# Three buffers for a unit's first weights, and the fourth chunk's routing spread over more units, in the first expert layer of an eight-block network

## The chip, the cores and the metric

The kernel runs on one core of one Trainium2 chip. A core has five engines with their own instruction queues: TensorE (PE, matmuls, with a separate row PEld for weight loads), VectorE (DVE), ScalarE (ACT), GpSimd (POOL) and SyncE (SP, which here only issues DMAs). They wait for one another by semaphores. The metric is the device time of one launch in microseconds (us), lower is better.

## The reference

Four pairs of attention and feed-forward layers work on 32 x 128 = 4096 tokens of width D = 128. The change lies in the first feed-forward layer, which mixes, normalises and routes each token to the best 2 of 8 experts:

```python
n = layer_norm(x, g1, be1)
x = res + n + (n @ mix_w + mix_b)
res = x
n = layer_norm(x, g2, be2)
probs = softmax(n @ router_w)
topw, topi = top_k(probs, 2)
combine = sum(one_hot(topi, E) * topw[..., None], axis=1)
h = silu(einsum('td,edf->tef', n, w1) + b1)
y = einsum('tef,efd->ted', h, w2) + b2
out = res + einsum('te,ted->td', combine, y)
```

## The kernel before

`routed_ffn` computes only the chosen experts. The 32 blocks of 128 tokens form four chunks of 8 blocks (chunks 0 to 3), and two chunks form a part, so that there are two parts. For a chunk, the routing is: VectorE scales the rows (`scale`), TensorE turns them (`turn_z`) and multiplies them by the mixing weights (`mix`), VectorE adds, takes statistics (`mix`, `statistics_1`), GpSimd makes the inverse deviation (`inverse_deviation`), VectorE normalises (`add_x1`, `normalise`, which writes the tile `r`), TensorE turns r (`turn_r`) and makes the logits (`logits`), VectorE and ScalarE make the softmax and pick two experts (`below_max`, `exponent`, `choose_first`, `choose_second`), TensorE counts the tokens before each (`count`), and VectorE makes of this the row of each token (`locate`). GpSimd then scatters the rows of r to these slots in device memory (`scatter`, 16 indirect DMAs for a chunk; those of chunks 2 and 3 wait after every four for the earlier ones to land).

When both chunks of a part are located, `table(p)` works out on VectorE which expert and which rows each unit of the part has. A unit is 256 slots of one expert; a part has 23 units, so there are 46 in all (0 to 45). `out_rows(c)` works out from where the results of chunk c are to be gathered.

A unit u costs: a load of its rows `xe` by SP (`load`, issued 5 units ahead, six buffers; the first load of a part waits for `table_done` and for all the part's scatters to land), a turn on TensorE (`turn_slots`), a copy to `xT` on ScalarE, a copy of the expert's first weights to the tile `w1_u` on VectorE (`copy_w1`, which reads the expert's number into a register first), the matmuls of `hidden` into h_bank, the activation on ScalarE, the matmuls of `result` into the single bank `y_bank`, and on VectorE `copy_y`, which adds the bias and writes `ye`; SP stores it. `result(u)` waits until `copy_y(u-1)` has left the bank. `hidden(u)` waits for `copy_w1(u)`.

The order on each engine is written out by hand. Routing of chunks 0 to 2 comes first (the head, HEAD = 3). `table(0)` and `copy_w1(0)`, `copy_w1(1)` stand in VectorE's queue between the routing of chunk 1 and that of chunk 2. Then comes the loop over units. In turn u of it TensorE does `hidden(u+1)`, `turn_slots(u+3)`, a piece of chunk 3's routing, `result(u)`; VectorE does `copy_w1(u+2)`, `copy_y(u)`, and then a piece of chunk 3's routing:

```python
for u in range(last_unit):
    if u + 2 < last_unit:
        expert[u + 2] = copy_w1(u + 2)
    copy_y(u, expert[u])
```

The pieces go by turn: `scale` in 0, `mix` and `statistics_1` in 2 and 3, both `add_x1` and `normalise` in 4, `turn_r` in 5, `logits` and `below_max` in 6, the choices in 7 and 8, `count` and `locate` in 9 (LAG), `table(1)` and `out_rows(0)` in 10, `out_rows(1)` in 11, `out_rows(2)` and `out_rows(3)` in 21 and 22. From turn 25 on VectorE also adds gathered results of part 0. What is left of the gathering is done in the attention layer that follows.

Of the kernel before, what the change touches and what calls it, by code (L numbers as in the profile page):

```python
# [1502 lines left out]
def routed_ffn(nc, core, name, w1, w1_loaded, w2_dram, b1, router_w, norms, mix_w, mix_b_dram, b2_dram, slots_in, slots_out, late):  # L1503
# [14 lines left out]
    LAG = 9  # L1518
# [11 lines left out]
    with ctx:  # L1530
# [58 lines left out]
        w1_u = [sb(f"w1_u{i}", [D, FC * 128]) for i in range(2)]  # L1589
# [94 lines left out]
        def _(pool):  # L1684
# [60 lines left out]
            scatter(2, 0, 8)  # L1745
            inverse_deviation(3)
            scatter(2, 8, 2 * RT)
# [4 lines left out]
        def _(dve):  # L1752
# [93 lines left out]
            def table(p):  # L1846

                first, last = PARTS[p]
                n, at = unit_counts[p], first_units[p]
                per_u = lambda v: v[:, None, :].to_broadcast([S, n, NE])  # L1850
                per_e = lambda v: v[:, :, None].to_broadcast([S, n, NE])
                numbers = core.iota_units[:, 0:n]
                hit = passed[:, 0:n, :]
                own.link(dve.tensor_tensor(held[:, :], base[:, last, :], begins[:, p, :], ALU.subtract))
                own.did(dve.tensor_scalar(lim[:, :], held[:, :], -float(UT), 0.0, ALU.add, ALU.max))
                own.link(dve.tensor_tensor(square[:, :, :], held[:, :, None].to_broadcast([S, NE, MOST]),
                                           steps[:, None, :].to_broadcast([S, NE, MOST]), ALU.is_gt))
                own.link(dve.tensor_reduce(units[:, :], square[:, :, :], AX.X, ALU.add))
                own.link(dve.tensor_tensor(square[:, :, 0:NE], upto[:, :, :],
                                           units[:, None, :].to_broadcast([S, NE, NE]), ALU.mult))  # L1860
                own.link(dve.tensor_reduce(ends[:, :], square[:, :, 0:NE], AX.X, ALU.add))
                own.link(dve.tensor_tensor(hit, per_u(ends[:, :]), per_e(numbers), ALU.is_le))
                own.link(dve.tensor_reduce(which[:, 0:n], hit[:, :, 0:NE - 1], AX.X, ALU.add))
                own.link(dve.tensor_tensor(hit, hit, per_u(ends[:, :]), ALU.mult))
                own.link(dve.tensor_reduce(begun[:, 0:n], hit[:, :, 0:NE - 1], AX.X, ALU.max))
                own.did(dve.tensor_copy(expert_of[:, at:at + n], which[:, 0:n]))
                own.did(dve.tensor_tensor(begun[:, 0:n], numbers, begun[:, 0:n], ALU.subtract))
                own.link(dve.tensor_tensor(hit, per_u(core.iota8[:, :]), per_e(which[:, 0:n]), ALU.is_equal))
                own.link(dve.tensor_tensor(hit, hit, per_u(lim[:, :]), ALU.mult))
                own.link(dve.tensor_reduce(row[:, 0:n], hit, AX.X, ALU.add))  # L1870
                own.did(dve.tensor_scalar(which[:, 0:n], which[:, 0:n], float((last - first) * REGION),
                                          float(first * NE * REGION), ALU.mult, ALU.add))
                own.link(dve.scalar_tensor_tensor(row[:, 0:n], begun[:, 0:n], float(UT), row[:, 0:n], ALU.mult, ALU.min))
                own.link(dve.tensor_tensor(row[:, 0:n], row[:, 0:n], which[:, 0:n], ALU.add))
                own.link(dve.tensor_copy(row_of[:, at:at + n], row[:, 0:n]))
                own.did(dve.scalar_tensor_tensor(terms[:, p, 2, :], units[:, :], float(UT), lim[:, :], ALU.mult, ALU.subtract))
                own.did(dve.tensor_tensor(terms[:, p, 1, :], lim[:, :], begins[:, p, :], ALU.add))
                own.link(dve.tensor_tensor(terms[:, p, 0, :], ends[:, :], units[:, :], ALU.subtract))
                own.did(dve.tensor_scalar(terms[:, p, 2, :], terms[:, p, 2, :], -float(UT), None, ALU.add))
                own.link(dve.scalar_tensor_tensor(terms[:, p, 0, :], terms[:, p, 0, :], float(UT), begins[:, p, :],  # L1880
                                                  ALU.mult, ALU.subtract))
                dve.sem_inc(table_done, 1)
# [17 lines left out]
            def copy_w1(u):  # L1900
                dve.wait_ge(table_done, part_of_unit[u] + 1)
                e = dve.value_load(expert_of[0:1, u:u + 1], min_val=0, max_val=NE - 1)
                if u >= 2:
                    dve.wait_ge(h_ready, 2 * (u - 1))
                dve.tensor_copy(w1_u[u % 2][:, :], w1[:, bass.ds(e * (FC * 128), FC * 128)]).then_inc(w1_copied, 1)
                return e
# [39 lines left out]
            for c in range(HEAD):  # L1946
                for g in (2 * c, 2 * c + 1):
                    mix(g)
                    statistics_1(g)
                add_x1(2 * c)  # L1950
                add_x1(2 * c + 1)
                statistics(2 * c + 2)
                normalise(2 * c)
                normalise(2 * c + 1)
                statistics(2 * c + 3)
                below_max(c)
                if c + 1 < HEAD:
                    scale(2 * c + 2)
                choose_first(c)
                choose_second(c)  # L1960
                if c + 1 < HEAD:
                    scale(2 * c + 3)
                locate(c)
                if c + 1 == PARTS[0][1]:
                    table(0)
                    dve.wait_ge(w1_loaded, 16 * NE)
                    expert = {0: copy_w1(0), 1: copy_w1(1)}
            dve.wait_ge(b2_loaded, 16)
            for u in range(last_unit):
                if u + 2 < last_unit:  # L1970
                    expert[u + 2] = copy_w1(u + 2)
                copy_y(u, expert[u])
                for c in BEGIN:
# [7 lines left out]
                    if since == 4:  # L1981
                        add_x1(2 * c)
                        normalise(2 * c)
                        add_x1(2 * c + 1)
                        normalise(2 * c + 1)
                    if since == 6:
                        below_max(c)
                    if since == 7:
                        choose_first(c)
                    if since == 8:  # L1990
# [18 lines left out]
        def _(act):  # L2009
# [50 lines left out]
            for u in range(last_unit):  # L2060
# [4 lines left out]
                for c in BEGIN:  # L2065
# [4 lines left out]
                    if since == 5:  # L2070
                        copy_r(2 * c)
                        copy_r(2 * c + 1)
                    if since == 6:
                        exponent(c)

        @block.tensor
        def _(pe):
# [102 lines left out]
            for u in range(last_unit):  # L2180
# [4 lines left out]
                for c in BEGIN:  # L2185
# [925 lines left out]
```

## Time and profile before

| | |
|---|---|
| median of 3 runs | 1486.42 us (1482.06 to 1490.42) |
| profiled execution, its own time | 1486.32 us |
| its span in the trace | 1484.5 us |
| TensorE busy | 1184.3 us (80% of the span) |
| VectorE busy | 991.8 us (67%) |
| ScalarE busy | 667.6 us (45%) |
| GpSimd busy | 537.8 us (36%) |
| mean granted TensorE clock | 0.886 |

Times in the rows are us from the span's start. A busy share is a mean over stages with different limits, so the stage of the change has to be read by itself. "Granted clock" is the share of TensorE's full clock that it was given. The first expert layer begins at about 232 us; its unit loop on TensorE goes from about 332 to 527 us. In a timeline row the bracket tells how long the engine was idle before the instruction and what ended the wait.

### The profile page before, as it was taken

What the parts mean: (1) busy time and instruction counts of PE and PEld (TensorE: products, weight loads), DVE (VectorE), ACT (ScalarE), POOL (GpSimd) and SP (SyncE); (2) the same over time, 40 slices, a digit from 0 to 9 for tenths busy, and PEclk for the clock granted to TensorE, in tenths of its full rate; (3) what the DMA queues carried; (4) which work ended last, traced back from release to release, by engine and by line L of the source; (5) the groups of instructions that cost most, each with busy time, mean ns of one, the idle gap of its engine ahead of it and who ended that gap; (6) DMA issues with size and microseconds to landing.
All of it is one profiled execution on the core that took longest, in us unless ns stands there. A gap on an engine that the chain in (4) does not pass through costs nothing. (4 is left out here: it accounts for less than half of the span.)

```text
span 1484.5 us, 34946 instructions
## 1 busy us (share of the span) xinstructions
PE 1184.3 (80%) x11154; PEld 926.2 (62%) x11154; DVE 991.8 (67%) x2920; ACT 667.6 (45%) x1423; POOL 537.8 (36%) x590
## 2 busy tenths in 40 slices
PE   2799994349899957789987879999799956399991
PEld 1577773238799934566674456677477746389991
DVE  3699885564533346989974678889477777756552
ACT  1377771115455503346554546666243343144440
POOL 2323302663305256635411233431121124752554
PEclk9999995559999966889988989999799988599996
DMA  7887733012223248534532086674200042133442
GB/s 179 211 212 196 186 105 127 29 51 65 78 79 106 85 119 205 135 100 130 155 91 51 19 191 157 152 170 106 85 1 0 0 150 64 54 119 107 147 141 74
DMA packets 138979, 164.58 MB, mean 111 GB/s; under 512 B 15309, under 2 KB 118755, under 8 KB 131729
## 3 DMA queue, kind: packets, MB, share of 16 engines
q1 hardware_dynamic: 130664, 146.62, 36.7%
q0 software_dynamic: 8192, 16.46, 4.0%
q8 instruction: 60, 0.98, 0.3%
q14 instruction: 63, 0.51, 0.1%
HBM read 111.98 MB, written 51.38 MB: 110 GB/s over the span
## 5 line engine op out<-in xcount | busy, mean ns | idle before, releaser
L586 DVE TENSOR_REDUCE A_neg_max<-A_s_bank 128x4 f32<-128x512 f32 x384 | 253.4, 688 | 45.0 <-PE A_s_bank L725 34.5
L448 ACT ACTIVATE A_probsT<-A_st_bank 128x512 f32<-128x512 f32 x384 | 222.2, 602 | 37.9 <-PE A_st_bank L738 36.9
L725 PE MATMUL A_s_bank<-A_k_stack,A_q_stack 72*128 72x128 bf16 x1536 | 158.9, 229 | 37.3 <-DVE A_neg_max L586 23.6
L738 PE MATMUL A_st_bank<-A_q_stack,A_k_stack 128*128 128x128 bf16 x1536 | 153.4, 224 | 7.0 <-DVE A_q_stack L602 6.2
L738 PEld LDWEIGHTS A_st_bank<-A_q_stack,A_k_stack 128*128 128x128 bf16 x1536 | 113.0, 104 | 51.7 <-issue 42.3
L725 PEld LDWEIGHTS A_s_bank<-A_k_stack,A_q_stack 72*128 72x128 bf16 x1536 | 107.2, 102 | 51.7 <-DVE A_neg_max L586 34.1
L752 PE MATMUL A_pv_bank<-A_probsT,A_v_pad 128*32 128x128 f32 x3072 | 128.3, 285 | 0.1
L2043 ACT ACTIVATE E_h<-E_h_bank,w_L_b 128x256 f32<-128x256 f32 x184 | 77.0, 472 | 82.0 <-PE E_h_bank L2143 80.8
L2143 PE MATMUL E_h_bank<-E_xT,E_w_u 128*128 128x256 f32 x368 | 91.4, 394 | 6.1 <-issue 6.1
L2155 PE MATMUL E_y_bank<-E_w,E_h 128*128 x736 | 90.3, 276 | 2.2 <-ACT E_h L2043 1.0
L752 PEld LDWEIGHTS A_pv_bank<-A_probsT,A_v_pad 128*32 128x32 f32 x3072 | 74.6, 111 | 23.5 <-issue 2.2
L2155 PEld LDWEIGHTS E_y_bank<-E_w,E_h 128*128 128x128 f32 x736 | 85.9, 192 | 3.3 <-issue 3.2
L461 ACT COPY A_outT<-A_pv_bank 128x512 f32<-128x512 f32 x99 | 58.0, 586 | 65.9 <-PE A_pv_bank L752 65.8
L2417 POOL DMA_INDIRECT E_yg<-slots_out,E_index_out x64 | 61.5, 960 | 63.9 <-DMA slots_out<-E_ye 29.5
L1912 DVE TENSOR_TENSOR E_ye<-E_y_bank,E_b 128x256 f32<-128x256 f32 x46 | 19.5, 424 | 95.2 <-PE E_y_bank L2155 95.1
L1714 POOL DMA_INDIRECT routed_in<-E_r,E_index x64 | 63.3, 989 | 51.7 <-DVE E_index L1844 27.6
L310 POOL TENSOR_TENSOR A_split_r<-A_k_f,A_k_parts 128x512 f32<-128x512 f32 (+1 forms) x21 | 26.1, 1242 | 151.0 <-ACT A_k_parts L472 75.4
L2402 POOL DMA_INDIRECT slots_in<-E_xn,E_index x64 | 64.0, 999 | 44.1 <-issue 16.9
L2143 PEld LDWEIGHTS E_h_bank<-E_xT,E_w_u 128*128 128x128 f32 x368 | 69.4, 199 | 14.9 <-issue 6.6
L602 DVE COPY A_q_stack<-A_max_rows 32x2048 bf16<-32x2048 bf16 x96 | 70.0, 729 | 2.7
L767 PE MATMUL A_t_bank<-ident,A_outT 128*128 128x128 f32 x396 | 66.6, 293 | 4.8 <-ACT A_outT L461 4.8
L2565 DVE COPY E_w_u<-exp_w 128x512 f32 x53 | 23.6, 448 | 59.9 <-PE E_v_bank L2779 52.3
(371 smaller groups left out, 2658.5 us busy)
## 6 DMA issues: line engine op xcount, KB each, us to landing
A_q_stack<-q_scratch SPq DMA_DIRECT2D x48, 576.0 KB
A_k_stack<-k_scratch SPq DMA_DIRECT2D x32, 576.0 KB
q_scratch<-A_q_parts SPq DMA_DIRECT2D x48, 192.0 KB
A_k_stack<-k_scratch SPq DMA_DIRECT2D x48, 192.0 KB
E_xe<-slots_in SPq DMA_DIRECT2D x53, 128.0 KB
slots_out<-E_ye SPq DMA_DIRECT2D x53, 128.0 KB, 1.7
A_ctxT<-in_ctxT SPq DMA_DIRECT2D x24, 256.0 KB, 10.0
k_scratch<-A_k_parts SPq DMA_DIRECT2D x32, 192.0 KB
```

Source lines behind the costliest of these rows:

```text
L448: act.activation(probsT[n % 2][:, c * HQ:(c + 1) * HQ, :], st_bank[c % 2][:, :].rearrange("k (a q) -> k a q", a=HQ), ACT.Exp, scale=scale) ...
L586: dve.tensor_reduce(neg_max[:, c * HQ:(c + 1) * HQ], s_bank[c % 2][:, :].rearrange("q (a k) -> q a k", a=HQ), AX.X, ALU.max, negate=True). ...
L602: dve.tensor_copy(q_stack[n // 2 % 4][MAX_ROWS, 0:BY_DVE, n % 2 * S:(n % 2 + 1) * S], max_rows[n % 2][MAX_ROWS, None, :].to_broadcast([2 * ...
L725: last = pe.matmul(s_bank[c % 2][:, a * S:(a + 1) * S], q_stack[slot][0:COMBO, h, at:at + S], k_stack[slot][0:COMBO, h, at:at + S], start= ...
L738: last = pe.matmul(dst, k_stack[slot][:, h, at:at + S], q_stack[slot][:, h, at:at + S], start=True, stop=spread)
L752: last = pe.matmul(pv_bank[a * VW:(a + 1) * VW, c * S:(c + 1) * S], v_pad[p][:, n % GB, h % vheads, :], probsT[n % 2][:, h, :], start=True ...
L767: last = pe.transpose(t_bank[:, a * S:(a + 1) * S], outT[:, a, :], core.ident[:, :])
L1714: pool.indirect_dma_start(out=slots_in[:, :], out_offset=bass.IndirectOffsetOnAxis(index[:, k, b:b + 1], 0), in_=r[:, b, :], in_offset=Non ...
L2043: last = act.activation(h[u % 2][:, f, :], h_bank[(2 * u + q) % HB][:, f % 2 * UT:(f % 2 + 1) * UT], ACT.Silu, bias=b1[:, bass.ds(e * FC + ...
L2143: last = pe.matmul(dst, w1_u[u % 2][:, f * 128:(f + 1) * 128], xT[u % 3][:, :], start=True, stop=True)
L2155: last = pe.matmul(y_bank[:, j * D:(j + 1) * D], h[u % 2][:, f, j * S:(j + 1) * S], w2[:, bass.ds(e * (FC * D) + f * D, D)], start=(f == 0 ...
L2402: pool.indirect_dma_start(out=slots_in[:, :], out_offset=bass.IndirectOffsetOnAxis(index[:, k, b:b + 1], 0), in_=xn[:, b, :], in_offset=No ...
```

## The change

The weights tile `w1_u` gets three buffers, `copy_w1` runs three units ahead of `copy_y` in place of two, and three copies in place of two stand in the head. The wait of a copy is for the same turn's `hidden` as before. Of chunk 3, the second `add_x1` and `normalise` go to turn 5, and each later step of the routing goes one turn later, up to `locate` in turn 10. `table(1)` is cut in three pieces for turns 11, 12 and 13; `out_rows` of the four chunks go to turns 14, 15, 20 and 21. GpSimd issues 12 in place of 8 scatters of chunk 2 ahead of chunk 3's inverse deviation. No arithmetic is added or taken away. The operations of `table` are the same, in the same order.

```diff
@@ -1515,7 +1515,8 @@
-    LAG = 9
+    LAG = 10
+    WBUF = 3
@@ -1586,7 +1587,7 @@
-        w1_u = [sb(f"w1_u{i}", [D, FC * 128]) for i in range(2)]
+        w1_u = [sb(f"w1_u{i}", [D, FC * 128]) for i in range(WBUF)]
@@ -1742,9 +1743,9 @@
             scale_of_z(3)
-            scatter(2, 0, 8)
+            scatter(2, 0, 12)
             inverse_deviation(3)
-            scatter(2, 8, 2 * RT)
+            scatter(2, 12, 2 * RT)
@@ -1843,7 +1844,7 @@
-            def table(p):
+            def table(p, pieces=(0, 1, 2)):
...
+                if 0 in pieces:
+                    own.link(dve.tensor_tensor(held[:, :], base[:, last, :], begins[:, p, :], ALU.subtract))
...
+                    own.link(dve.tensor_reduce(ends[:, :], square[:, :, 0:NE], AX.X, ALU.add))
+                if 1 in pieces:
+                    own.link(dve.tensor_tensor(hit, per_u(ends[:, :]), per_e(numbers), ALU.is_le))
...
+                    own.did(dve.tensor_tensor(begun[:, 0:n], numbers, begun[:, 0:n], ALU.subtract))
+                if 2 in pieces:
+                    own.link(dve.tensor_tensor(hit, per_u(core.iota8[:, :]), per_e(which[:, 0:n]), ALU.is_equal))
...
+                    dve.sem_inc(table_done, 1)
@@ -1900,9 +1904,9 @@
-                if u >= 2:
-                    dve.wait_ge(h_ready, 2 * (u - 1))
-                dve.tensor_copy(w1_u[u % 2][:, :], w1[:, bass.ds(e * (FC * 128), FC * 128)]).then_inc(w1_copied, 1)
+                if u >= WBUF:
+                    dve.wait_ge(h_ready, 2 * (u - WBUF + 1))
+                dve.tensor_copy(w1_u[u % WBUF][:, :], w1[:, bass.ds(e * (FC * 128), FC * 128)]).then_inc(w1_copied, 1)
@@ -1964,11 +1968,11 @@
-                    expert = {0: copy_w1(0), 1: copy_w1(1)}
+                    expert = {u: copy_w1(u) for u in range(WBUF)}
             dve.wait_ge(b2_loaded, 16)
             for u in range(last_unit):
-                if u + 2 < last_unit:
-                    expert[u + 2] = copy_w1(u + 2)
+                if u + WBUF < last_unit:
+                    expert[u + WBUF] = copy_w1(u + WBUF)
                 copy_y(u, expert[u])
@@ -1978,28 +1982,22 @@
-                    if since == 4:
-                        add_x1(2 * c)
-                        normalise(2 * c)
-                        add_x1(2 * c + 1)
-                        normalise(2 * c + 1)
-                    if since == 6:
+                    if since in (4, 5):
+                        add_x1(2 * c + since - 4)
+                        normalise(2 * c + since - 4)
+                    if since == 7:
                         below_max(c)
-                    if since == 7:
+                    if since == 8:
                         choose_first(c)
-                    if since == 8:
+                    if since == 9:
                         choose_second(c)
                     if since == LAG:
                         locate(c)
-                if u == BEGIN[NR - 1] + LAG + 1:
-                    table(1)
-                    out_rows(0)
-                if u == BEGIN[NR - 1] + LAG + 2:
-                    out_rows(1)
-                if u == BEGIN[NR - 1] + LAG + 12:
-                    out_rows(2)
-                if u == BEGIN[NR - 1] + LAG + 13:
-                    out_rows(3)
+                located = u - BEGIN[NR - 1] - LAG
+                if located in (1, 2, 3):
+                    table(1, (located - 1,))
+                if located in (4, 5, 10, 11):
+                    out_rows((4, 5, 10, 11).index(located))
@@ -2067,10 +2065,10 @@
-                    if since == 5:
+                    if since == 6:
                         copy_r(2 * c)
                         copy_r(2 * c + 1)
-                    if since == 6:
+                    if since == 7:
                         exponent(c)
@@ -2140,7 +2138,7 @@
-                        last = pe.matmul(dst, w1_u[u % 2][:, f * 128:(f + 1) * 128], xT[u % 3][:, :],
+                        last = pe.matmul(dst, w1_u[u % WBUF][:, f * 128:(f + 1) * 128], xT[u % 3][:, :],
@@ -2189,10 +2187,10 @@
-                    if since == 5:
+                    if since == 6:
                         turn_r(2 * c)
                         turn_r(2 * c + 1)
-                    if since == 6:
+                    if since == 7:
                         logits(2 * c)
                         logits(2 * c + 1)
```

## Rows read from the trace of the kernel before

**Rows 1.** the stretches view of TensorE: start:end, length, PE busy (matmuls), granted clock

```profile
393.00:399.00 6.00, 0.34 (x4) 0.73 0.14 44
399.00:403.00 4.00, 3.77 (x11) 0.55 0.30 98
403.00:450.00 47.00, 47.00 (x330) 1.00 0.27 81
```

**Rows 2.** the timeline of TensorE: start, us, line, what, count, idle before it

```profile
357.81 1.95 PE L2155 MATMUL E_y_bank<-E_w,E_h 128*128 x16
...
362.82 0.66 PE L2105 MATMUL E_t_bank<-ident,E_r 128*128 128x128 f32 x4 [0.67 <-DVE E_r L1800]
...
365.09 2.05 PE L2155 MATMUL E_y_bank<-E_w,E_h 128*128 x16 [0.20 <-issue]
...
391.39 1.95 PE L2155 MATMUL E_y_bank<-E_w,E_h 128*128 x16
399.23 3.61 PE L2143 MATMUL E_h_bank<-E_xT,E_w_u 128*128 128x256 f32 x8 [5.89 <-issue]
402.67 0.38 PE L2132 MATMUL E_x_bank<-ident,E_xe 128*128 128x128 f32 x2
402.89 1.95 PE L2155 MATMUL E_y_bank<-E_w,E_h 128*128 x16
...
440.23 1.95 PE L2155 MATMUL E_y_bank<-E_w,E_h 128*128 x16
...
448.02 1.95 PE L2155 MATMUL E_y_bank<-E_w,E_h 128*128 x16
```

**Rows 3.** the timeline of VectorE after unit 10's result copy

```profile
390.09 0.16 DVE L1854 TENSOR_TENSOR E_held<-E_base,E_begins 128x8 f32<-128x8 f32 x1
...
391.44 0.35 DVE L1862 TENSOR_TENSOR E_passed<-E_ends,iota_units 128x184 f32<-128x184 f32 x1
...
393.09 0.34 DVE L1868 TENSOR_TENSOR E_passed<-iota,E_which 128x184 f32<-128x184 f32 x1
...
395.86 0.63 DVE L1887 TENSOR_TENSOR E_weighed<-E_pick,E_terms 128x192 f32<-128x192 f32 x2
...
397.62 0.17 DVE L1896 TENSOR_TENSOR late_index<-E_chosen 128x16 uint32<-128x16 f32 x1
398.56 0.56 DVE L1905 COPY E_w_u<-exp_w 128x512 f32 x1 [0.78 <-DVE late_index L1896]
```

**Rows 4.** the timeline of VectorE, chunk 3's second sum and second r

```profile
362.46 0.69 DVE L1794 TENSOR_TENSOR x_sb<-x_sb,E_x 128x512 f32<-128x512 f32 x1
363.07 1.11 DVE L1800 TENSOR_SCALAR E_r<-E_x,E_mv,E_rstd 128x128 f32<-128x128 f32 x4
```

**Rows 5.** the timeline of VectorE around a lone out_rows

```profile
438.94 0.62 DVE L1887 TENSOR_TENSOR E_weighed<-E_pick,E_terms 128x192 f32<-128x192 f32 x2
...
442.33 0.42 DVE L1912 TENSOR_TENSOR E_ye<-E_y_bank,E_b 128x256 f32<-128x256 f32 x1 [0.26 <-PE E_y_bank L2155]
```

**Rows 6.** the timeline of all engines, first two weight copies

```profile
306.03 0.43 DVE L1905 COPY E_w_u<-exp_w 128x512 f32 x1 [1.27 <-issue]
...
306.80 0.43 DVE L1905 COPY E_w_u<-exp_w 128x512 f32 x1 [0.34 <-issue]
...
308.38 0.61 PE L2094 MATMUL E_m_bank<-E_mix_b,E_ones 65*128 65x512 bf16 x1 [6.54 <-DVEq L1782]
```

**Rows 7.** the timeline of GpSimd: deviation and last scatter of chunk 3

```profile
359.16 0.23 POOL L1703 TENSOR_SCALAR E_rstd<-E_mv 128x8 f32<-128x8 f32 x1 [18.18 <-DVE E_mv L1790]
...
410.58 0.96 POOL L1714 DMA_INDIRECT routed_in<-E_r,E_index  x1 [0.30 <-issue]
```

**Rows 8.** the timeline of the DMA queue, load of unit 23

```profile
425.28 0.34 SPq L1654 DMA_DIRECT2D E_xe<-routed_in  x1
```

**Rows 9.** the view of the scatter's line: ns min/median/max; landing in us

```profile
L1714 POOL DMA_INDIRECT routed_in<-E_r,E_index x48: 956/962/1185, 299.7 to 410.6; - x48
...
DMA to landing us min/median/max: 2.2/2.2/3.0
```

More of the change, by code:

```diff
@@ L1853, in table @@
                 hit = passed[:, 0:n, :]
[L1854 to L1881, printed above, removed]
@@ L1882, in table @@
-                dve.sem_inc(table_done, 1)
+                if 0 in pieces:
+                    own.link(dve.tensor_tensor(held[:, :], base[:, last, :], begins[:, p, :], ALU.subtract))
+                    own.did(dve.tensor_scalar(lim[:, :], held[:, :], -float(UT), 0.0, ALU.add, ALU.max))
+                    own.link(dve.tensor_tensor(square[:, :, :], held[:, :, None].to_broadcast([S, NE, MOST]),
+                                               steps[:, None, :].to_broadcast([S, NE, MOST]), ALU.is_gt))
+                    own.link(dve.tensor_reduce(units[:, :], square[:, :, :], AX.X, ALU.add))
+                    own.link(dve.tensor_tensor(square[:, :, 0:NE], upto[:, :, :],
+                                               units[:, None, :].to_broadcast([S, NE, NE]), ALU.mult))
+                    own.link(dve.tensor_reduce(ends[:, :], square[:, :, 0:NE], AX.X, ALU.add))
@@ new lines, in table @@
+                if 1 in pieces:
+                    own.link(dve.tensor_tensor(hit, per_u(ends[:, :]), per_e(numbers), ALU.is_le))
+                    own.link(dve.tensor_reduce(which[:, 0:n], hit[:, :, 0:NE - 1], AX.X, ALU.add))
+                    own.link(dve.tensor_tensor(hit, hit, per_u(ends[:, :]), ALU.mult))
+                    own.link(dve.tensor_reduce(begun[:, 0:n], hit[:, :, 0:NE - 1], AX.X, ALU.max))
+                    own.did(dve.tensor_copy(expert_of[:, at:at + n], which[:, 0:n]))
+                    own.did(dve.tensor_tensor(begun[:, 0:n], numbers, begun[:, 0:n], ALU.subtract))
@@ new lines, in table @@
+                if 2 in pieces:
+                    own.link(dve.tensor_tensor(hit, per_u(core.iota8[:, :]), per_e(which[:, 0:n]), ALU.is_equal))
+                    own.link(dve.tensor_tensor(hit, hit, per_u(lim[:, :]), ALU.mult))
+                    own.link(dve.tensor_reduce(row[:, 0:n], hit, AX.X, ALU.add))
+                    own.did(dve.tensor_scalar(which[:, 0:n], which[:, 0:n], float((last - first) * REGION),
+                                              float(first * NE * REGION), ALU.mult, ALU.add))
+                    own.link(dve.scalar_tensor_tensor(row[:, 0:n], begun[:, 0:n], float(UT), row[:, 0:n], ALU.mult, ALU.min))
+                    own.link(dve.tensor_tensor(row[:, 0:n], row[:, 0:n], which[:, 0:n], ALU.add))
+                    own.link(dve.tensor_copy(row_of[:, at:at + n], row[:, 0:n]))
+                    own.did(dve.scalar_tensor_tensor(terms[:, p, 2, :], units[:, :], float(UT), lim[:, :], ALU.mult, ALU.subtract))
+                    own.did(dve.tensor_tensor(terms[:, p, 1, :], lim[:, :], begins[:, p, :], ALU.add))
+                    own.link(dve.tensor_tensor(terms[:, p, 0, :], ends[:, :], units[:, :], ALU.subtract))
+                    own.did(dve.tensor_scalar(terms[:, p, 2, :], terms[:, p, 2, :], -float(UT), None, ALU.add))
+                    own.link(dve.scalar_tensor_tensor(terms[:, p, 0, :], terms[:, p, 0, :], float(UT), begins[:, p, :],
+                                                      ALU.mult, ALU.subtract))
+                    dve.sem_inc(table_done, 1)
```

## The prediction

> **What bounds the kernel now.** The page's busy shares don't settle this: they are means over eight blocks with different limits. I went to the timeline of TensorE in the first expert layer. From unit 12's result (402.89) to unit 22's (440.23) its rows follow each other with no idle time: 37.34 / 10 = 3.73 us for a unit, made of `hidden`, `turn_slots` and `result` [rows 2]. So in this stretch TensorE sets the pace, and only time in which it stands still, or runs at a lower clock, can be won. The result of unit n is called y(n) below. Three intervals are longer than 3.73 by more than the chunk's own matmuls.
>
> - y(11) to y(12): 402.89 - 391.39 = 11.50. Ahead of `hidden(13)` TensorE is idle for 5.89 [rows 2].
> - y(4) to y(5): 365.09 - 357.81 = 7.28. Here TensorE waits for r of chunk 3 (0.67 before the first turn shown) [rows 2].
> - y(22) to y(24): 448.02 - 440.23 = 7.79, against 7.47 for two units [rows 2].
>
> The first wait is labelled "issue". VectorE's timeline says what it is. In turn 10 it begins `table(1)` at 390.09 and `out_rows(0)` at 395.86, whose last instruction starts at 397.62; only then comes the copy of unit 13's weights, 398.56 to 399.12 [rows 3]. `hidden(13)` starts at 399.23, 0.1 later [rows 2]. The stretches view adds the second half of the cost: from 393 to 399 the granted clock is 0.73 on average and from 399 to 403 it is 0.55, near the lower of the two levels (1.2 of 2.4 GHz); from 403 to 450 it is 1.00 [rows 1]. The matmuls of `hidden(13)` therefore take 402.67 - 399.23 = 3.44 until the next turn starts. The stall costs 11.50 - 3.73 = 7.77 in all, not 5.89.
>
> **The change part by part.**
>
> *Table and row indices.* The burst is cut into 391.44 - 390.09 = 1.35, 393.09 - 391.44 = 1.65, 395.86 - 393.09 = 2.77 and some 1.93 for `out_rows(0)` (395.86 to 397.79) [rows 3], each in a turn of its own. Are they short enough? The two-buffer kernel shows a burst of about this size: `out_rows(2)` in turn 21 starts at 438.94 [rows 5], and its two turns together lose only 0.32 [rows 2]. With copies two units ahead a burst of 1.9 is at the edge. A third buffer gives the copy another 3.73, so the copy is no longer what limits. What remains is the single `y_bank`: `result(u+2)` needs `copy_y(u+1)`. After the burst of 438.94 the copy of y(22) starts at 442.33, 0.42 long [rows 5]; it could end as late as y(23) is due, 440.23 + 3.73 = 443.96. That leaves 443.96 - 442.75 = 1.2 more, so a burst up to 1.9 + 1.2 = 3.1 is free. The longest piece is 2.77. It fits by 0.3 to 0.4, and I take no stall: saved 7.77. Bounds: the 5.89 of idle time alone (the clock falls for another reason) less 0 to 1 of a stall behind piece 3, so 4.9, to 7.77.
>
> *Copies three ahead, elsewhere.* The 0.32 of turns 21 and 22 goes (now 20 and 21). The lone copy delay ahead of `hidden(6)` sits in the 7.28 below.
>
> *Second r in turn 5, turns of r in turn 6.* A slot turn of two transposes takes 402.89 - 402.67 = 0.22 [rows 2], so the eight of `turn_r` need about 0.88; they are moved, not removed. The 7.28 holds 3.73 + 0.88 + 2.67 of waits. Is r there in time now? In turn 6 the turns are due 3.73 after y(5) starts. VectorE behind y(5): 1.95 for the result, 0.42 for the copy, 0.61 for the sum (363.07 - 362.46), 1.11 for r [rows 2, 4, 5], with two hops of about 0.1: 4.3. The first group of four turns (0.44) is already served by turn 4, so the second is wanted at 4.17. About 0.1 short, with a little issue time behind it: I charge 0.2, with bounds of 0 and 0.87 (the row's idle 0.67 again plus the 0.20 of issue ahead of y(5)). Saved 2.67 - 0.2 = 2.47.
>
> *The third copy in the head.* It stands in VectorE's queue ahead of `mix(4)`. TensorE waited 6.54 for that at 308.38 [rows 6], and GpSimd's inverse deviation, the last scatters of chunk 1 and so the first unit loads hang on the same chain. Nothing hides it. The second copy came 306.80 - 306.03 = 0.77 after the first [rows 6]; cost 0.77. Bounds: 0.43 for a bare copy, 1.70 if it also shows the 1.27 gap of the first [rows 6].
>
> *Routing a turn later.* The same matmuls at full clock on TensorE, 0 in themselves. Their exposed waits (logits, exponent, `count`) keep the same distances in turns, so I carry them over unchanged. What becomes late is chunk 3's scatter, on which the first load of part 1 waits. Before, `locate` was in turn 9; y(9) started two units before y(11), at about 383.9, and the last scatter was issued at 410.58 [rows 7], 26.7 later. Now it follows y(10), which started at 391.39 - 3.73 = 387.66 and comes 2.47 - 0.77 = 1.7 earlier, at 386.0: last scatter 412.7, landed 2.2 later [rows 9], at 414.9. The load of unit 23 was issued at 425.28 [rows 8]; with 2.47 + 7.77 - 0.77 = 9.47 less, 415.8. So it is just free, and the unit's turn is due only before y(20), which was at 402.89 + 8 x 3.73 = 432.8: 432.8 - 0.22 - 9.47 = 423.1. With 3.0 for the landing (the longest landing in rows 9, taken as the bound for a load too), scatters may end up to 423.1 - 3.0 - 414.9 = 5.2 later before TensorE waits. Cost 0, cover 5.2.
>
> *GpSimd's four earlier scatters of chunk 2.* They take 4 x 1.27 at their spacing of 0.96 and 0.30 idle, some 5, and fall into the 18.18 for which GpSimd stood idle ahead of chunk 3's inverse deviation at 359.16 [rows 7]. Cost 0; without that cover the 5 would delay r and turn 6.
>
> On this chip a copy that meets a scatter shows little: the 48 scatters take 956 to 1185 ns with a median of 962 [rows 9], while the copy that met one at 398.56 took 0.56 in place of 0.42 or 0.43 [rows 3, 6]. If each of the 7 copies made during chunk 3's scatters held one for its whole 0.56, they would end 3.9 later, inside the cover of 5.2; that is what gives the second rival below its chance. The Trainium skill, SBUF — State Buffer, "Who interferes with whom", speaks against this mix: it has a two-port VectorE copy and a GpSimd instruction lock each other out for the whole instruction. By that rule the 3.9 would be real and the sum the same.
>
> **The sum.** 7.77 + 2.47 + 0.32 - 0.77 = 9.8. The profiled execution took 1486.32, of which 1.8 lies around its span of 1484.5, and the part after the layer follows its end as before: 1486.32 - 9.8 = 1476.5. The median of the runs is 0.1 above the profiled one, so both lead to the same forecast. 0.5% is 7.4 us, about what a measurement of this kernel can tell from no change.
>
> **The rivals.**
>
> - *The stall moves to the result bank.* `copy_y(u+1)` behind piece 3 comes too late, and perhaps also behind a piece and an `out_rows` whose gap is longer than shown. For: the margin is only 0.3 to 0.4. Against: three of four bursts are under 2. Up to 1 for each of four bursts: 1477.5 to 1480.5. Chance 0.10.
> - *Chunk 3 arrives late and the kernel gets slower.* Scatters spaced wider, by contention with the copies that now run beside them, hold the load of unit 23 and all behind it. It costs from the moment the last landing slips by 5.2; it eats the whole gain at 15.0, and makes the kernel slower by over 0.5% at 22.4, that is 1.4 for each of the 16 scatters on top of 0.96. For: `locate` is later and the units before are faster. Against: the longest of 48 scatters is 1.19 [rows 9], 16 x 0.22 = 3.6, inside the cover. 1477 to 1495. Chance 0.05, of it 0.03 slower by over 0.5%.
> - *The change doesn't do what it says, or it is given back later.* The layer ends earlier, but the attention layers shift against DMA and clock phases, or TensorE's clock falls somewhere else. For: the clock fell once within an idle time of six [rows 1], and the runs of before spread over 8. Against: nothing in the layer's end depends on the absolute time, and `hidden(13)` follows its copy by 0.1 [rows 2, 3]. Half to all of the gain lost: 1481 to 1487. Chance 0.15.
>
> **How the numbers follow.** The forecast mechanism has 0.70, at 1476.5 with its own range of 1472 to 1481 (4.9 to 7.77 for the big stall, 0.43 to 1.70 for the copy, 0 to 0.87 for r, and the spread of a median). It is below 1479.0, the limit of 0.5%, in about 0.8 of its cases: 0.57. The bank rival adds 0.03, the late chunk and the given-back cases 0.03: faster 0.63. Slower by over 0.5%: 0.03 from the late chunk and 0.01 from the last rival. Same: the rest, 0.33. The range of 8 in 10 reaches into the second and third rivals: 1471 to 1484.5.
>
> **What the profile after would show.** Right: y(n) at 3.73 distance from unit 10 on with no idle time of several us at turns 11 to 15, granted clock 1.00 from about 340 to 525; y(4) to y(5) at 3.73, and y(5) to y(6) at 4.6 to 5.5; the first `hidden` 0.8 later; the stage's end about 9.8 earlier. Wrong: an idle time ahead of `result` behind piece 3, with a release by `copy_y`; turns of unit 23 waiting for a DMA; or a first unit later by well over 1. The forecast fails as a whole if the gain is in the layer but not at the end.

## The result, and the profile after

The changed kernel takes 1474.7 us (median of 5 runs, 1472.96 to 1476.99) against 1486.42 before: ratio 0.9931 on record, 95% interval 0.9905 to 0.9956 (the two medians alone give 0.9921). So it is faster beyond the noise, but the interval ends just short of the 0.5% that the prediction took as its limit. The forecast was 1476.5. Its profiled execution took 1473.61, with a span of 1471.7.

Much of a comparison of whole spans is the spread between executions, so the layer is measured by itself: from SP's first load in it (233.71 here, 232.09 before) to the first matmul of the attention layer behind it (524.73 here, 533.59 before). That is 291.02 against 301.50 us, and 290.90 against 301.25 in a second profile of each: 10.4 less. The other 2.3 by which the first two spans differ lie outside the layer.

The stretches view of TensorE, columns as in [rows 1]. The granted clock, 0.73 and 0.55 before, is 1.00 in all four stretches:

```profile
345.00:393.00 48.00, 46.53 (x334) 1.00 0.23 71
393.00:399.00 6.00, 6.00 (x43) 1.00 0.34 109
399.00:403.00 4.00, 4.00 (x31) 1.00 0.38 120
403.00:450.00 47.00, 47.00 (x328) 1.00 0.31 94
```

TensorE's timeline, to be held against [rows 2]. y(4) starts at 359.37, and y(5) follows 3.73 later, at 363.10. The eight turns of r stand in the next interval (366.84), with only 0.20 of wait ahead of y(6) at 368.16. y(11) at 390.68, y(12) at 394.41 and y(13) at 398.15 follow at 3.73, as do all units where the stall of 5.89 was. y(22) to y(24) is 7.47. The turn of unit 23 is the row at 424.07:

```profile
359.37 1.95 PE L2153 MATMUL E_y_bank<-E_w,E_h 128*128 x16
...
363.10 1.95 PE L2153 MATMUL E_y_bank<-E_w,E_h 128*128 x16
...
366.84 1.12 PE L2103 MATMUL E_t_bank<-ident,E_r 128*128 128x128 f32 x8
368.16 2.05 PE L2153 MATMUL E_y_bank<-E_w,E_h 128*128 x16 [0.20 <-issue]
...
390.68 1.95 PE L2153 MATMUL E_y_bank<-E_w,E_h 128*128 x16
...
394.41 1.95 PE L2153 MATMUL E_y_bank<-E_w,E_h 128*128 x16
...
397.93 0.38 PE L2130 MATMUL E_x_bank<-ident,E_xe 128*128 128x128 f32 x2
398.15 1.95 PE L2153 MATMUL E_y_bank<-E_w,E_h 128*128 x16
...
424.07 0.38 PE L2130 MATMUL E_x_bank<-ident,E_xe 128*128 128x128 f32 x2
424.29 1.95 PE L2153 MATMUL E_y_bank<-E_w,E_h 128*128 x16
...
431.75 1.95 PE L2153 MATMUL E_y_bank<-E_w,E_h 128*128 x16
...
439.22 1.95 PE L2153 MATMUL E_y_bank<-E_w,E_h 128*128 x16
```

VectorE's timeline in turns 11 to 14, to be held against [rows 3]. Each piece of the table (393.12, 396.85, 400.59) is followed by one weights copy (L1909) and one result copy (L1916). The result copy behind the longest piece starts at 404.27 and ends at 404.69, while y(15) starts at 405.62: 0.93 to spare. Some 0.25 of that is needed between the end of such a copy and the result that waits for it (measured in table_whole below), so about 0.7 is free.

```profile
393.12 0.16 DVE L1856 TENSOR_TENSOR E_held<-E_base,E_begins 128x8 f32<-128x8 f32 x1
...
395.19 0.58 DVE L1909 COPY E_w_u<-exp_w 128x512 f32 x1 [0.78 <-DVE E_ends L1863]
396.51 0.42 DVE L1916 TENSOR_TENSOR E_ye<-E_y_bank,E_b 128x256 f32<-128x256 f32 x1 [0.74 <-PE E_y_bank L2153]
396.85 0.34 DVE L1865 TENSOR_TENSOR E_passed<-E_ends,iota_units 128x184 f32<-128x184 f32 x1
...
399.12 0.43 DVE L1909 COPY E_w_u<-exp_w 128x512 f32 x1 [0.49 <-issue]
400.24 0.42 DVE L1916 TENSOR_TENSOR E_ye<-E_y_bank,E_b 128x256 f32<-128x256 f32 x1 [0.70 <-PE E_y_bank L2153]
400.59 0.34 DVE L1872 TENSOR_TENSOR E_passed<-iota,E_which 128x184 f32<-128x184 f32 x1
...
402.88 0.16 DVE L1884 SCALAR_TENSOR_TENSOR E_terms<-E_terms,E_begins 128x8 f32<-128x8 f32 x1
403.93 0.43 DVE L1909 COPY E_w_u<-exp_w 128x512 f32 x1 [0.89 <-DVEq L1886]
404.27 0.42 DVE L1916 TENSOR_TENSOR E_ye<-E_y_bank,E_b 128x256 f32<-128x256 f32 x1
```

GpSimd's and SP's rows, to be held against [rows 7, 8]: the first scatter of chunk 3, the two with a long wait for earlier ones to land, the last, and the load of unit 23:

```profile
390.80 0.96 POOL L1715 DMA_INDIRECT routed_in<-E_r,E_index  x1 [22.38 <-DVE E_index L1845]
...
404.93 1.12 POOL L1715 DMA_INDIRECT routed_in<-E_r,E_index  x1 [3.11 <-DMA routed_in<-E_r,E_index]
...
412.68 1.16 POOL L1715 DMA_INDIRECT routed_in<-E_r,E_index  x1 [2.83 <-DMA routed_in<-E_r,E_index]
...
416.68 0.96 POOL L1715 DMA_INDIRECT routed_in<-E_r,E_index  x1 [0.30 <-issue]
```

```profile
420.38 0.34 SPq L1655 DMA_DIRECT2D E_xe<-routed_in  x1
```

The 16 scatters span 416.68 - 390.80 = 25.9 from the start of the first to that of the last. The load of unit 23 now waits for them: it is issued 3.7 after the last one starts, which is the distance that the first load of part 0 also keeps from the scatter that it waits for (325.61 to 329.27), and 3.7 ahead of its turn.

### The profile page after: what moved, and what is told of

It reads as the page before. It is cut to its first block and busy times, and to the rows that moved or that the text cites. A ratio compares the mean times of both kernels' runs of the same rounds, so it can differ in the third digit from the quotient of the medians.

```text
span 1471.7 us, 34934 instructions
## 1 busy us (share of the span) xinstructions
PE 1178.9 (80%) x11141; PEld 924.6 (63%) x11154; DVE 990.6 (67%) x2920; ACT 667.2 (45%) x1423; POOL 536.8 (36%) x590
## 5 line engine op out<-in xcount | busy, mean ns | idle before, releaser
L725 PE MATMUL A_s_bank<-A_k_stack,A_q_stack 72*128 72x128 bf16 x1536 | 158.6, 229 | 36.9 <-DVE A_neg_max L586 23.4
L1916 DVE TENSOR_TENSOR E_ye<-E_y_bank,E_b 128x256 f32<-128x256 f32 x46 | 19.5, 425 | 84.2 <-PE E_y_bank L2153 84.2
```

The source lines that it names most:

```text
L725: last = pe.matmul(s_bank[c % 2][:, a * S:(a + 1) * S], q_stack[slot][0:COMBO, h, at:at + S], k_stack[slot][0:COMBO, h, at:at + S], start= ...
```

## The experiments

The table gives, for every kernel run, some distances between results y(n) in us, the layer (as measured above) and what lies outside it. "y22-24" is for two units.

```
kernel                y4-5  y5-6  y9-10 y11-12 y12-13 y14-15 y19-20 y20-21 y22-24  y0-y44  layer   outside
before                7.28  5.54  3.83  11.50   3.74   3.73   3.73   3.74   7.79  183.48  301.50  1183.00
before_again          7.28  5.53  3.83  11.31   3.73   3.74   3.73   3.74   7.79  183.22  301.25  1178.95
changed               3.73  5.06  5.00   3.73   3.74   3.74   3.74   3.73   7.47  173.12  291.02  1180.68
after_again           3.74  5.05  4.99   3.74   3.73   3.74   3.73   3.74   7.47  173.12  290.90  1180.70
wbuf_only             7.28  6.91  3.84   8.35   5.97   3.73   3.73   3.73   7.47  183.55  301.83  1182.47
spread_only           4.18  5.06  4.98   3.74   3.73   4.61   3.73   3.74   7.59  175.19  293.01  1178.69
r_split_only          4.17  5.05  5.00   3.74  11.79   3.74   3.74   3.73   7.78  182.17  300.29  1178.31
table_whole           3.73  5.05  4.99   3.73   6.20   3.73   3.73   3.74   7.47  175.65  292.52  1179.38
third_copy_later      3.74  5.05  4.99   3.73   3.73   3.73   3.73   3.74   7.47  173.26  291.36  1182.14
six_more_copies       3.74  5.05  5.00   3.74   3.73   3.74   3.73   3.73   7.47  173.12  297.73  1182.87
scatters_as_before    3.74  5.05  4.99   3.74   3.73   3.73   3.74   3.73   7.47  173.10  291.11  1186.69
locate_4_later        3.73  5.06  3.83   3.74   3.73   3.81  14.31   5.44   7.47  184.58  301.07  1182.13
locate_1_later        3.74  5.05  3.83   3.81   3.74   3.74   3.89   3.83   7.47  172.43  288.65  1174.55
locate_1_later_timed  3.74  5.06  3.83   3.82   3.73   3.73   3.84   3.83   7.47  172.39  289.30  1178.80
```

Small differences in the layer have to be read with care. Leaving six_more_copies aside, the layer less y0-y44 is 117.8 to 118.3 in nine profiles, but 116.2 to 116.9 in four (table_whole, locate_4_later and both of locate_1_later). In these four `locate(1)` already ends about 1 earlier after the layer's first load than in the others, though nothing that their edits touch has run by then. So these 1 to 2 us are spread too, and the column y0-y44 is the one that tells the edits apart.

**The third buffer alone.**

```diff
 (the kernel before)
+    WBUF = 3          # w1_u, copy_w1, hidden and the head's copies by WBUF, as in the change
```

> The kernel before with the third weights buffer alone (copies three ahead, three copies in the head); chunk 3's routing, the table and the row indices stay where they were. Theory of the prediction (the burst of 7.7 us in turn 10 first makes the copy late, and with that cured the single result bank): hidden(13) no longer waits, but result(12) waits for the copy of y(11), which stands behind the burst: y(11) to y(12) falls from 11.50 to 8.1 to 9.0 us, the wait ahead of hidden(6) (0.36) and the 0.32 of turns 21 and 22 go, the head costs 0.77: the kernel 2.4 to 3.5 us faster than before. Rival (the buffer alone brings the gain, the spreading is for nothing): y(11) to y(12) at 3.73, some 8 us faster.

Ratio to before 0.9996 (0.9979 to 1.0014), layer 301.83 against 301.50 and 301.25: no gain to be seen. The first step is as forecast: y(12) comes after 8.35 in place of 11.50, and what releases it is the result copy, not the weights copy. But y(13) follows after 5.97, and y(5) to y(6) has grown from 5.54 to 6.91. Both are the clock. TensorE's timeline of this kernel, around y(12), then around y(5):

```profile
401.54 3.78 PE L2156 MATMUL E_y_bank<-E_w,E_h 128*128 x16 [4.45 <-DVE E_ye L1913]
405.11 2.35 PE L2144 MATMUL E_h_bank<-E_xT,E_w_u 128*128 128x256 f32 x8
```

```profile
363.32 0.66 PE L2106 MATMUL E_t_bank<-ident,E_r 128*128 128x128 f32 x4 [1.12 <-DVE E_r L1801]
364.72 0.84 PE L2106 MATMUL E_t_bank<-ident,E_r 128*128 128x128 f32 x4 [0.75 <-DVE E_r L1801]
365.58 3.41 PE L2156 MATMUL E_y_bank<-E_w,E_h 128*128 x16
```

and its stretches, clock in the column behind the busy time:

```profile
362.00:366.00 4.00, 2.10 (x12) 0.88 0.24 73
366.00:370.00 4.00, 4.00 (x22) 0.69 0.10 33
...
398.00:402.00 4.00, 0.46 (x2) 0.65 0.16 49
402.00:407.00 5.00, 5.00 (x23) 0.60 0.33 106
```

y(12) takes 405.11 - 401.54 = 3.57 from its start to the next matmul, twice the usual 1.79, and the matmuls of y(5) last 3.41 against 2.05 [rows 2]. The waits ahead of the turns of r, 1.12 and 0.75, were 0.67 and 0.76 in the kernel before, where the clock held in both profiles. y(4) to y(5) is the same 7.28: r was what was waited for, and the 0.20 of wait that the kernel before had ahead of hidden(6) only moved into the wait for r. The two intervals with the lower clock are 2.2 and 1.4 longer for it, which takes back what the buffer gained. So my forecast of 2.4 to 3.5 fell: it had priced the idle time and only up to 0.9 of clock. That the clock fell at y(5) here and not before rests on one profile of this kernel.

**The spreading alone.**

```diff
 (the changed kernel)
-    WBUF = 3
+    WBUF = 2
```

> The changed kernel with two weights buffers in place of three, so the spreading alone. Theory of the prediction (with copies two ahead a burst up to about 1.8 us is free): table pieces of 1.35 and 1.65 us cost nothing, the piece of 2.77 costs 1.0 to 1.2, each out_rows of 1.93 costs 0.1 to 0.2, the r burst of turn 4 at most 0.4; the head's 0.77 comes back. In the loop y(0) to y(44) 1.5 to 2.2 us longer than in the changed kernel, the whole 0.8 to 1.5 slower than it, 10 faster than before. Rival (without the third buffer the spreading only cuts the stall into several): y intervals of turns 11 to 15 of 4.5 to 6 each, the whole 4 us or more slower than the changed kernel.

Ratio 0.9945 (0.9925 to 0.9964). The loop is 175.19 - 173.12 = 2.07 longer than in the changed kernel: the longest piece of the table costs 0.88, the r burst 0.45, the out_rows 0.32 and less, and the two shorter pieces nothing. The rival falls: there are no five intervals of 4.5 to 6. The 0.8 of the head that was to come back did not. The interval of the ratio overlaps that of the changed kernel, so what the third buffer adds to the spreading is shown in the loop (2.07) and not in the kernel's time.

**The r steps alone.**

```diff
 (the kernel before)
-    LAG = 9
+    LAG = 10
...
-                    if since == 4:
+                    if since in (4, 5):
...
-                    if since == 5:
+                    if since == 6:
...
-                if u == BEGIN[NR - 1] + LAG + 12:
+                if u == BEGIN[NR - 1] + LAG + 11:
...
-                if u == BEGIN[NR - 1] + LAG + 13:
+                if u == BEGIN[NR - 1] + LAG + 12:
```

> The kernel before with chunk 3's steps moved as in the change (second sum and r in turn 5, turns of r in turn 6, each later step one turn later), but with two weights buffers, the four scatters where they were, and table(1) with out_rows(0) still in one turn. Theory of the prediction (this part is worth 2.47 with copies three ahead; with two, 0.4 of it stays because the r burst of turn 4 makes a copy late, as in the run with the spreading alone): y(4) to y(5) 4.1 to 4.2, y(5) to y(6) 5.06, the long interval stays at 11.3 to 11.5 one unit later; layer 1.9 to 2.3 shorter than before. Rival (the waits for r only move to turn 6): layer within 0.7 of before.

y(4) to y(7) falls from 16.64 to 14.76, by 1.9 as expected, but the long interval is 11.79, with 3.97 behind it, and takes 0.5 back. The layer is 1.0 to 1.2 shorter and not the 1.9 to 2.3 expected. Ratio 0.9987 (0.9967 to 1.0007), not to be told from 1. The edit's effect on the intervals that it touches is as expected; the long stall is not a fixed number, it was 11.31, 11.50 and 11.79 in three profiles.

**The whole table in one turn.**

```diff
 (the changed kernel)
-                if located in (1, 2, 3):
-                    table(1, (located - 1,))
+                if located == 1:
+                    table(1)
```

> The changed kernel with table(1) in one turn (turn 11), 5.8 us long, in place of three. Theory of the prediction (with three weights buffers the single result bank is the limit, a burst up to 3.1 us is free): y(12) to y(13) is 3.73 + 2.7 = 6.4 us with TensorE idle ahead of result, released by the copy of y; the clock may fall to its lower level in it and cost 0 to 1.9 more there or in the next interval. 2.7 to 4.6 slower than the changed kernel in the layer. Rival (the third buffer moves the limit by a whole unit, to 1.8 + 3.73 = 5.5): 0.3 us, nothing to be seen.

y(12) to y(13) is 6.20, 2.47 over a unit, released by the result copy; the theory said 2.7, the rival 0.3. TensorE's timeline and stretches of this kernel: after 2.30 of idle time the clock stays at 1.00, so almost nothing comes on top (y(13) to y(14) is 3.83).

```profile
398.02 0.38 PE L2130 MATMUL E_x_bank<-ident,E_xe 128*128 128x128 f32 x2
400.70 2.05 PE L2153 MATMUL E_y_bank<-E_w,E_h 128*128 x16 [2.30 <-DVE E_ye L1916]
```

```profile
396.00:400.00 4.00, 2.40 (x15) 1.00 0.11 33
400.00:404.00 4.00, 3.30 (x23) 1.00 0.35 115
404.00:410.00 6.00, 6.00 (x47) 1.00 0.43 135
```

Ratio 0.9949 (0.9927 to 0.9972). The loop is 2.5 longer than in the changed kernel. The layer is only 1.5 longer, below the 2.7 to 4.6 expected, because this is one of the four profiles with an early head. With 5.6 as the length of the burst (393.20 to 398.81) and 2.47 of stall, the free length is 3.1. The result copy that releases y(13) ends at 400.45, 0.25 ahead of it.

**The head: one copy out of it, six copies into it.**

```diff
 (the changed kernel)
-                    expert = {u: copy_w1(u) for u in range(WBUF)}
+                    expert = {u: copy_w1(u) for u in range(WBUF - 1)}
...
+            expert[WBUF - 1] = copy_w1(WBUF - 1)
             dve.wait_ge(b2_loaded, 16)
```

> The changed kernel with the third weights copy taken out of the head and put behind the routing of chunk 2, ahead of the unit loop, where VectorE is idle. Theory of the prediction (nothing hides the copy in the head): the wait of TensorE for mix(4)'s sum falls from 7.34 to 6.6 us, and y(0) comes 0.77 earlier after the layer's first instruction; the loop unchanged. Rival (the first unit's rows are what is waited for, and the copy was hidden): the same wait is shorter but y(0) keeps its distance from the layer's first instruction.

```diff
 (the changed kernel)
                     expert = {u: copy_w1(u) for u in range(WBUF)}
+                    for again in range(6):
+                        e = dve.value_load(expert_of[0:1, 2:3], min_val=0, max_val=NE - 1)
+                        own.link(dve.tensor_copy(w1_again[:, :], w1[:, bass.ds(e * (FC * 128), FC * 128)]))
```

> The changed kernel with six more weights copies into an unused tile behind the three of the head: nothing else. Theory of the prediction (the copies in the head lie on the chain): TensorE waits 6 x 0.77 = 4.6 us longer for mix(4)'s sum (each copy also waits for the one before, so up to 6.5), and y(0) comes later by the same. Rival (the chain through the scatters of chunk 1 and the first loads has slack): mix's wait grows by 4.6 or more, y(0) by at least 0.8 less.

TensorE's wait for mix(4)'s sum, in the changed kernel, with one copy less, and with six more:

```profile
311.19 0.61 PE L2092 MATMUL E_m_bank<-E_mix_b,E_ones 65*128 65x512 bf16 x1 [7.34 <-DVEq L1783]
```

```profile
308.44 0.61 PE L2093 MATMUL E_m_bank<-E_mix_b,E_ones 65*128 65x512 bf16 x1 [6.56 <-DVEq L1783]
```

```profile
319.32 0.61 PE L2096 MATMUL E_m_bank<-E_mix_b,E_ones 65*128 65x512 bf16 x1 [14.11 <-DVEq L1784]
```

The wait follows the copies: 7.34, 6.56, 14.11. The first unit's turn does not, at first. From `locate(1)`'s last instruction to that turn it is 30.0 in the changed kernel, 30.4 with one copy less, and 30.0 and 30.1 in the two profiles of the kernel before, but 36.9 with six more (6.8 for the 6.8 of longer wait). So of the two expectations for one copy less the rival holds (the copy was hidden), and six more are not hidden at all; they cost 1.1 each and not 0.77. How much a fourth copy would cost was not run. Where the 0.8 goes: the last scatter of chunk 1 is issued 0.8 earlier where two copies stand ahead, and lands 3.0 to 3.3 after its issue in all five such profiles; with three copies or nine it lands after 2.2, in the other nine. The first load waits for that landing. Why it lands later there stays open. Ratio of third_copy_later 0.9925 (0.9902 to 0.9948), of no use beyond the change.

**Chunk 3 later still.** `LAG` 10 of the changed kernel to 14, and to 11:

```diff
-    LAG = 10
+    LAG = 14
```

> The changed kernel with count and locate of chunk 3, and the table pieces and row indices behind them, four turns later (LAG 14 in place of 10), so its scatters come 4 x 3.73 = 14.9 us later. Theory of the late-chunk rival with the cover that the changed kernel's profile shows (load of unit 23 issued at 420.38, its turn due at 427.80, landing up to 3.3: 4.1 left): TensorE waits 14.9 - 4.1 = 10.8 (9.5 with a landing of 2.0) ahead of the turn of unit 23, and 1 to 2 more by the lower clock behind it; 10 to 13 slower than the changed kernel, about as slow as the one before. Rival (the loads of units 23 and up don't depend on these scatters in a way that matters): no wait there.

```diff
-    LAG = 10
+    LAG = 11
```

> The changed kernel with count, locate, table pieces and row indices of chunk 3 one turn later (LAG 11). In the changed kernel's profile the load of unit 23 is issued at 420.38 and its turn is due at 424.07; in the run with four turns more the turn came 2.16 after the load, so 424.07 - 420.38 - 2.16 = 1.5 us of cover are left. Theory: the scatters come 3.73 later, TensorE waits about 2.2 (0 to 2.9, as the scatters take 23 to 26 us from first to last) ahead of the turn of unit 23. Rival (the cover of 5.2 worked out in the prediction holds): no wait.

With four turns more, load and turn of unit 23:

```profile
429.16 0.34 SPq L1655 DMA_DIRECT2D E_xe<-routed_in  x1
```

```profile
431.32 0.69 PE L2130 MATMUL E_x_bank<-ident,E_xe 128*128 128x128 f32 x2 [9.78 <-DMA E_xe<-routed_in]
432.17 3.65 PE L2153 MATMUL E_y_bank<-E_w,E_h 128*128 x16 [0.17 <-issue]
```

TensorE stands still for 9.78 and the unit is 10.58 late; its result runs at the lower clock (5.44 to the next, 1.7 lost). Ratio 1.0008 (0.9979 to 1.0037): the whole gain is gone. The second rival's mechanism is real: with four turns more it costs all that the change gained. The expectation's size was right by luck: I had put unit 23's turn at 427.80; it is at 424.07, which left 1.5 and not 4.1, while the scatters took 23.1 here against 25.9.

With one turn more:

```profile
418.26 0.34 SPq L1655 DMA_DIRECT2D E_xe<-routed_in  x1
```

```profile
420.94 0.38 PE L2130 MATMUL E_x_bank<-ident,E_xe 128*128 128x128 f32 x2
421.31 2.05 PE L2153 MATMUL E_y_bank<-E_w,E_h 128*128 x16
```

The turn follows the load by 2.7, and the intervals ahead of y(20) and y(21) lose 0.25 together, not the 2.2 expected: the scatters took 23.9 from first to last. What I had not expected is a gain: y(9) to y(12) is 11.6 in place of 12.6. `count` now stands a turn behind the choice of experts. In the changed kernel it starts right behind that choice, 0.3 late, and 0.51 of idle time follow ahead of the result; with one turn more both are gone. As this single execution took 1465.0, less than any of the changed kernel, the same kernel was run six times more:

> The same kernel as the run before this one (count and locate one turn later than in the changed kernel), timed in five rounds, as its one look took 1465.0, less than any run of the changed kernel. Theory (what the unit intervals show: count no longer waits for the choice of experts, 0.9 less in turns 10 and 11, and 0.25 more at units 20 and 21 by the later loads; the other 8 us of that look lie outside the layer and are the spread between executions): y(0) to y(44) 172.4 again, time 0 to 1.5 us below the changed kernel's 1474.7 to 1476.0, ratio to before 0.991 to 0.993. Rival (moving the count changes something outside the layer): time below 1470, outside the layer below 1176 again.

1472.3 us (1469.84 to 1475.39), ratio 0.9911 (0.9894 to 0.9928); y(0) to y(44) 172.39 and the layer 289.30. The layer shows 0.7 of gain in the loop; the interval overlaps that of the changed kernel (0.9905 to 0.9956), so that it is faster than the changed kernel is not shown. The rival falls: most of what made the first execution so short lies outside the layer (1174.55 there, 1178.80 here).

**Scatters as before, and both kernels once more.**

```diff
 (the changed kernel)
-            scatter(2, 0, 12)
+            scatter(2, 0, 8)
             inverse_deviation(3)
-            scatter(2, 12, 2 * RT)
+            scatter(2, 8, 2 * RT)
```

> The changed kernel with the split of chunk 2's scatters as before: 8 ahead of chunk 3's inverse deviation in place of 12. Theory of the prediction (the four fall into GpSimd's idle time, cost and gain 0): unit intervals of the changed kernel to 0.02 us, y(0) to y(44) 173.1, GpSimd's idle time ahead of the deviation 17 to 18 in place of 10.64. Rival (fewer scatters ahead leave more behind, which collide with unit loads and delay the turns of units 6 to 9): y(5) to y(9) longer by 0.2 or more.

> The kernel before, unchanged, for one more profile: how far the layers outside the change differ between two executions. Theory: the unit intervals of the first expert layer are the same to 0.02 us (11.50 and 7.28 for the two long ones, up to 0.9 less or more where the clock changes), while the time outside this layer differs by 1 to 4 us between executions. Rival (the layers behind the change depend on where it ends, so the other 2.4 us that the changed kernel's profile is shorter are the change's): the time outside the layer is the same to 0.5 us.

> The changed kernel, unchanged, for one more profile and one more comparison. Theory: y(0) to y(44) again 173.1 us to 0.3, the layer 290 to 292, and what lies outside the layer anywhere in the 1178 to 1183 that the kernels so far showed, unrelated to the change; ratio to before between 0.990 and 0.996. Rival (the 2.3 us outside the layer by which the changed kernel's first profile is shorter belong to the change): outside the layer 1180.7 to 0.5.

The scatters' split moves no interval by more than 0.02; GpSimd's idle time ahead of the deviation is 17.05 against 10.64. The two kernels repeat the loop to 0.3 and 0.00. Outside the layer the kernel before gave 1183.00 and 1178.95, so the rival of before_again falls. The changed kernel gave 1180.68 and 1180.70, which fits both the theory and the rival of after_again and does not decide between them. But it lies between the two values of the kernel before, and the 14 profiles together give 1174.6 to 1186.7, so nothing speaks for a part of the 2.3 that belongs to the change. The second timing of the changed kernel gave 0.9932 (0.9905 to 0.9958).

## Why the prediction was right

- **The big stall: 7.77 forecast, 7.77 measured** (11.50 to 3.73; against the second profile of the kernel before it is 7.6). The forecast was that nothing of the stall would be left, and that is what came. Most of it is the spreading: alone it gets 8.3 of the loop's 10.4, and the third buffer adds the last 2.1. The buffer alone leaves the result bank as the limit, the clock falls as before, and nothing is won.
- **The limit of the result bank: 3.1 forecast, 3.1 measured** in table_whole. The longest piece kept some 0.7 and not 0.3 to 0.4: by itself it takes 2.45 (400.59 to 403.04), not the 2.77 that reaches to the start of out_rows behind it. A little luck is in the 3.1. The working left out that the copy of 442.33 had itself waited 0.26 for its matmuls [rows 5], and that a result needs some 0.25 behind such a copy; the two cancel. The first rival did not happen.
- **Turns 21 and 22: 0.32, and 0.32.**
- **r: 2.47 forecast, 2.32 measured** over y(4) to y(7) (16.64 to 14.32).
- **The third copy in the head: 0.77 forecast, 0 measured.** This is the term that was off, and the sign "the first `hidden` 0.8 later" did not appear: y(0) comes 106.6 after the layer's first load in the changed kernel and 106.7 in the one before. The step "nothing hides it" was wrong: the chain of VectorE and GpSimd did move by 0.8, but the last scatter's landing took 0.8 less. Six more copies delay the first unit by as much as they delay the mixing, so the rest of the chain is as tight as I said.
- **The cover of chunk 3: 5.2 forecast, about 1.5 left.** The mechanism was right and the size was not. I had kept the scatters' spacing of the kernel before (22.8 from first to last); they span 25.9, as they wait 3.11 and 2.83 us for landings. I had also let the load follow the start of the last scatter by 2.2, the landing alone, where it follows by 3.7. These are 4.6; 0.8 comes back, as a load lands in 2.2 and not in the 3.0 taken as its bound, and the turn is due 0.1 later. The longer span goes with unit loads that no longer pause: it is 22.8 in all four profiles that keep the long stall there, and 23.1 to 25.9 in the ten that do not. Which transfer holds up a scatter was not traced. No unit was late by it in the changed kernel.
- **The clock** was right by the rows of before, but only because I took the whole interval. In wbuf_only almost the same waits brought it down where before they did not.
- **Sum:** 10.4 in the layer against 9.8; the difference is the head's 0.77, less 0.15 on r. The rest of the 11.7 between the medians is the spread outside, so that the forecast of the whole time came within 1.8 us is in part luck.

The Trainium skill, SBUF — State Buffer, "Who interferes with whom", says that a VectorE copy in a two-port mode and a GpSimd instruction lock each other out: the one that issues first holds the shared ports for its whole length, and the other is fully blocked. This trace does not agree for these scatters. In the changed kernel the copy below runs in its usual 0.43 while the scatter of 390.80 is under way (0.96 long); the one at 395.19 takes 0.58 beside the scatter of 394.58; and the 16 scatters of chunk 3 take 954 to 1164 ns. The time is lost in the waits for landings, not in the instructions.

```profile
391.16 0.43 DVE L1909 COPY E_w_u<-exp_w 128x512 f32 x1 [0.63 <-PE E_h_bank L2141]
```

## What to carry to other kernels

Price a stall by the distance between two like results, not by the idle time the profile names: here 5.89 of idle time was 7.77. When a buffer is added, ask which single buffer the same burst blocks next, and make the burst shorter than that one allows. When a step is moved later, redo the spacing of its DMAs with the traffic that will run beside them.

## What was not expected of the hardware

- TensorE's clock after short idle times: it held at 1.00 through 2.30 of idle time (table_whole) and through waits of 0.67 and 0.76 close together (before), and fell behind waits of 1.12 and 0.75 (wbuf_only, 365.6). Behind a stall of 4.45 (wbuf_only, y(12)) it cost 2.2 more. Each of these but the second is from one profile, so how long a stall has to be is not shown.
- The landing of an indirect scatter took 2.2 us in most cases, but a wait for four of them grew from 1.53 to 3.1 us, 3.4 in scatters_as_before, while loads and stores of 128 KB went on beside them.
- The last scatter ahead of the first load landed in 3.0 to 3.3 in the five profiles with two weights copies in VectorE's queue, and in 2.2 in the nine with three or more. The cause stays open.
